# A cross-attention and mixture-of-experts kernel: the next chunk's first key unit moved to the end of each slot

## The chip, the cores and the metric

The kernel runs on one core of one Trainium2 chip. The metric is the device time of one execution in microseconds (us). The core's engines are TensorE (PE in the profile; PEld is its weight load), VectorE (DVE), ScalarE (ACT), GpSimd (POOL) and SyncE (SP), which here only issues DMAs.

## The reference, cut to what matters

```python
x = x + xattn(layernorm(x), ctx, ctx, mask, ...)   # x (64, 128, 128), ctx (64, 120, 128), 16 heads of 8
x = x + ffn(layernorm(x), Wr, W1, b1, W2, b2)       # 8 experts, hidden 512, best 2 of 8 by softmax

def xattn(q_in, k_in, v_in, mask, ...):
    q, k, v = (split_heads(t @ W + b) for ...)
    score = einsum('bhqd,bhkd->bhqk', q, k) / sqrt(8)
    attn = softmax(where(mask, -1e30, score), axis=-1)
    return merge_heads(attn @ v) @ Wo + bo
```

## The kernel before

The work has two phases. The first, up to about 570 us, is attention, the router, and the sorting of rows to experts. The second (the tiles of the expert network) and the final sum are not touched by the change.

**Chunks and slots.** The 64 sequences are taken two at a time: 32 chunks. All engines walk through the same list of slots, `for s in range(-2, 34)`, written out in full. In slot n an engine works on several chunks at once: chunk c = n+1 has its keys and queries projected and the largest score of each query found; chunk n gets its exponentials and its product with the values; chunk n-1 gets its second half's output and the router's logits; chunk n+2 is loaded, normalised and split. The order within a slot is the order of the code on each engine; each engine runs its queue strictly in that order and the engines meet by semaphores.

**A chunk's projections.** There are four units: `project(c, 0)` and `project(c, 1)` make the keys of head groups 0, 1 and 2, 3; `project(c, 2)` and `(c, 3)` make the queries. Each is six matmuls (L1208 to L1210, fp32 split in a high and a low part) into one of three PSUM banks (`wide[u % 3]`) that the scores use too. On ACT `halve(c, u)` (L1039) scales and shifts the bank into `part`. On DVE `unsplit(c, u)` (L695) subtracts `part` from the bank; the result goes to `ks` (keys) or `qs` (queries). When `unsplit` of units 0 and 1 is done, SP copies `ks` in four DMAs (L346, `kb<-ks`) into the block layout `kb`. Only when those have landed can `by_query(c, 0)` (L1247) make the first scores of chunk c, from which DVE takes the maxima (`best`, L700).

**The end of a slot.** After the eighth product with the values (`weigh`, L1269) PE transposes the maxima (L1373) when the last `best` is done; DVE negates and splits them (L868, L870) and SP sends them to a row of `qb` (L365), which the next slot's first `by_key` (L1257) waits for. PE then makes the router's logits (L1381), from which DVE takes the best experts (L878 to L884), and ACT the exponentials `tope` (L1114). DVE also ends the row positions of the router (`posi`, L777), on which POOL's next scatter (L531) waits. ACT's `take_heads(s, 1)` (L1130) copies the second half's heads out of PSUM to `ots1`; the next slot's `turn_heads(s, -1)` on PE (L1229) transposes that copy and so waits for it.

**The start of a slot on PE**: `project(c, 0)`, `turn_heads`, `project(c, 1)`, `turn_on` (L1234, waits for DVE's L660 and L664), `project(c, 2)`, `by_key` twice.

**POOL** runs in each slot, in order: the scatter that waits for `posi`, the mask pair (L556), the output bias, a scatter, the split of chunk n+2's context (L570, L572), a root, a scatter, and in slots 3 to 18 also the split of expert weights (L590, L592).

Of the kernel before, what the change touches and what calls it, by code (L numbers as in the profile page):

```python
# [51 lines left out]
def moe_attention(nc, x, ctx, mask, maskT, Wq, bq, Wk, bk, Wv, bv, Wo, bo, Wr, W1, b12, W2, out):  # L52
# [24 lines left out]
    with ExitStack() as st:  # L77
# [210 lines left out]
        def exists(s, back):  # L288

            return s is None or 0 <= s + back < NCH  # L290
# [345 lines left out]
        def _(dve):  # L636
# [39 lines left out]
            def slot(s, n):  # L676
                c = s + 1
# [4 lines left out]
                    dve.wait_ge(b_full, s.count(8))  # L682
                    dve.wait_ge(pv_done, s.count(8))

                def unsplit(u):

                    dve.wait_ge(w_part, c.count(4, u + 1))
                    gs = slice(2 * (u % 2), 2 * (u % 2) + 2)
                    if u < 2:
                        views = ks[k][:, gs, :], *(w[:, 0:2 * KW].rearrange("p (g n) -> p g n", g=2)[:, :, 0:K2]  # L690
                                                   for w in (wide[u % 3], part[u % 2]))
                    else:
                        views = qs[k][:, :, gs, :], *(w[:, 0:2 * N2].rearrange("p (g b q) -> p b g q", g=2, b=2)
                                                      for w in (wide[u % 3], part[u % 2]))
                    v.tensor_tensor(*views, ALU.subtract).then_inc(w_free, 1)  # L695
# [86 lines left out]
                    normalise((s, -1), False)  # L782
                route(0)
                if exists(n, 1):
                    unsplit(0)
                    route(1)
                    unsplit(1)
                    if n == 0:
                        output_bias()
                else:  # L790
                    route(1)
# [29 lines left out]
                    dve.wait_ge(ln_chain, (s + 3).count(LN, 2))  # L821
                    v.tensor_scalar(ve[:, :], mv[:, :, 1], EPS, None, ALU.add).then_inc(ln_chain, 1)  # L822
                if exists(n, 1):
                    unsplit(2)
                    unsplit(3)
                if exists(n, 2):
                    f = s + 2
                    dve.wait_ge(hx_done, f.count(1, 1))
# [35 lines left out]
                if exists(n, 1):  # L864

                    dve.wait_ge(nm_full, c.count(1, 1))
                    nsrc = small[0][0:J * G * 2, 0:S]
                    v.tensor_scalar(negm[k][:, 0, :], nsrc, -1.0, None, ALU.mult).then_inc(nm_split, 1)  # L868
                    dve.wait_ge(nm_split, c.count(2, 1))
                    v.scalar_tensor_tensor(negm[k][:, 1, :], nsrc, -1.0, negm[k][:, 0, :], ALU.mult, ALU.subtract).then_inc(nm_split, 1)  # L870
                if exists(n, -1):

                    alone(dve, rl_full, s.count(1))
                    lg = small[1][:, 0:2 * E].rearrange("p (b e) -> p b e", b=2)
                    if n != 1:
                        alone(dve, routed, s.count(1, -1))
                    for b in range(2):
                        last = v.max(top[:, b, :], lg[:, b, :])  # L878
                    last.then_inc(top_max, 1)
                    alone(dve, top_max, s.count(1))  # L880
                    for b in range(2):
                        last = v.max_index(tidx[:, b, :], top[:, b, :], lg[:, b, :])
                    last.then_inc(rl_taken, 1)
                    v.tensor_tensor(topd[:], top[:], top[:, :, 0:1].to_broadcast([P, 2, E]), ALU.subtract).then_inc(top_sub, 1)  # L884
# [120 lines left out]
        def _(act):  # L1005
# [3 lines left out]
            def clear(blocks, spec):  # L1009
                dst = flat(blocks, spec).rearrange("p (a n) -> p a n", a=8)  # L1010
                return dst, zeros[:, 0:dst.shape[2]].rearrange("p (a n) -> p a n", a=1).to_broadcast(list(dst.shape))
# [38 lines left out]

            def slot(s, n):
                c = s + 1
                if exists(n, 1):
                    halve(c, 0, n)
                    halve(c, 1, n)
                if exists(n, -1):
                    take_on(s, -1)
                for t in range(8):
                    if t < 7:
                        exponentials(s, t, n)  # L1060
                    if t == 6:
                        if exists(n, -1):
                            m = s + -1
                            act.wait_ge(ln_chain, (s + 3).count(7, 7))
                            if exists(n, -2):
                                act.wait_ge(x2t_full, s.count(1, -1))
                            if exists(n, -5):
                                act.wait_ge(scat[m.phase], m.turns(64, -64))
                            for b in range(2):
                                last = a.activation(rows[m.phase][:, b, 0, 0:D], xres[:, 2 * n - 2 + b, :], ACT.Identity,  # L1070
                                                    bias=shift[:, 2 + b:3 + b], scale=ys[1][:, 2 + b:3 + b])
                            last.then_inc(ln2_done, 1)
                        if exists(n, 3):
                            norm_x(s, n)
                        exponentials(s, 7, n)
                    if t in (0, 1) and exists(n, 1):
                        halve(c, t + 2, n)
                    if t == 4 and exists(n, 0):
                        take_heads(s, 0, n)
                    if t == 2 and exists(n, 1):  # L1080
                        if n == -1:
                            act.wait_ge(vs_zero, 4)
                        act.wait_ge(v_full, c.count(1, 1))
                        if n is None or n >= 1:
                            act.wait_ge(pv_done, s.count(8))
                        a.activation(vs[c.parity][:, :, :, 0:DH].rearrange("p b h d -> p (b h) d"),
                                     small[0][0:KL, 0:2 * D].rearrange("p (b h d) -> p (b h) d", b=2, h=H), ACT.Copy).then_inc(v_taken, 1)
                    if t == 2 and exists(n, 2):

                        f = s + 2  # L1090
                        act.wait_ge(tx_full, f.count(1, 1))
                        if n is None or n >= 0:
                            act.wait_ge(w_full, s.count(12, 4))
                        elif n == -2:
                            act.wait_ge(one_set, 1)
                        a.activation(xcTh[f.parity][:, 0:N2], small[1][:, 0:N2], ACT.Identity, bias=one[:, 0:1]).then_inc(hx_done, 1)
                    if t == 6 and exists(n, 0):
                        take_on(s, 0)
                    if t == 6 and exists(n, -1):

                        act.wait_ge(x2t_full, s.count(1))
                        if n != 1:
                            act.wait_ge(rl_full, s.count(1, -1))
                        a.activation(x2s[:, :], small[0][:, 0:N2], ACT.Copy).then_inc(x2t_taken, 1)
                if n == -2:
                    a.activation(*clear(qb[0], "p b g j q"), ACT.Copy).then_inc(blk_zero, 1)
                if n == -1:
                    a.activation(*clear(kb[1], "p g j n"), ACT.Copy).then_inc(blk_zero, 1)
                    a.activation(*clear(qb[1], "p b g j q"), ACT.Copy).then_inc(blk_zero, 1)
                if exists(n, 0):  # L1110
                    take_heads(s, 1, n)
                if exists(n, -1):
                    act.wait_ge(top_sub, s.count(1))
                    a.activation(tope[:].rearrange("p b e -> p (b e)"), topd[:].rearrange("p b e -> p (b e)"), ACT.Exp).then_inc(top_exp, 1)  # L1114
# [62 lines left out]
        def _(pe):  # L1177
# [58 lines left out]
            def project_out(s, k):  # L1236
                pe.wait_ge(ont_taken, s.count(2, k + 1))
                t_.matmul(small[1][:, 0:D], onT[:, :], wraw[:, 3, :], start=True, stop=True).then_inc(wo_full, 1)
# [34 lines left out]
            def slot(s, n):  # L1273
                c = s + 1
                if n == NCH + 1:
                    turn_x(At(-1, 3), -1, 1)
                if exists(n, 1):
                    project(c, 0, n)
                if n == 0:
                    output_bias()  # L1280
# [19 lines left out]
                for t in range(8):  # L1300
# [61 lines left out]
                        last.then_inc(x2t_full, 1)  # L1362
                    if exists(n, 0) and t == 6:
                        project_out(s, 0)
                    if exists(n, 1) and t == 7:
                        pe.wait_ge(w_free, c.count(12, 12))
                        if n == -1:
                            pe.wait_ge(v_taken, 1)
                        elif n == 0:
                            pe.wait_ge(on_done, 1)  # L1370
                        else:
                            pe.wait_ge(x2t_taken, s.count(1))
                        t_.transpose(small[0][0:J * G * 2, 0:S], mx[:].rearrange("p b g j -> p (b g j)"), ident[:, :]).then_inc(nm_full, 1)  # L1373
# [111 lines left out]
```

## Time and profile before

| | |
|---|---|
| time, median of 3 runs | 906.77 us (905.45 to 907.99) |
| time of the profiled execution | 904.83 us |
| span of the profiled execution | 903.0 us |
| PE busy | 760.7 us (84%) |
| DVE busy | 670.0 us (74%) |
| ACT busy | 621.2 us (69%) |
| POOL busy | 477.3 us (53%) |

The span is the time from the first to the last instruction of the profiled execution; 1.8 us more lie around it in the time measured. A busy share is a mean over stages that are limited in different ways, so it doesn't say what a change within a slot is worth.

### The profile page before, as it was taken

The numbers are of one execution on the slowest core, as the hardware profiler recorded it, in microseconds if no ns is written. First come the engines' busy times: TensorE is split into PE (matmuls) and PEld (weight loads), VectorE is DVE, ScalarE is ACT, GpSimd is POOL, SyncE is SP. The second block draws the span as 40 slices with busy tenths as digits, with TensorE's granted clock in tenths as the row PEclk, the third lists the DMA queues.
The fourth block names the chain that finished last, engine by engine and source line by source line (L and its number), as shares of the span: only waits on it lengthen the run. The fifth ranks groups of instructions, "written<-read, shape, count | busy, mean of one in ns | idle before, by whom it ended". The sixth has DMA issues, their size and how long they took to land.

```text
span 903.0 us, 19629 instructions
## 1 busy us (share of the span) xinstructions
PE 760.7 (84%) x5606; PEld 546.5 (61%) x5606; DVE 670.0 (74%) x2133; ACT 621.2 (69%) x1131; POOL 477.3 (53%) x715
## 2 busy tenths in 40 slices
PE   2689899998998988889988889759999999999700
PEld 1456555655655655656665665448888888888500
DVE  3568888888888887888887887557777777777536
ACT  4667677677677676667776677458888888888500
POOL 4122665565565565454453453453777777767720
PEclk9599999999999999999999999759999999999955
DMA  5333355455445445334243233388877777877059
GB/s 157 75 83 73 98 129 150 115 135 153 115 127 154 116 130 145 102 93 100 72 100 92 70 85 80 141 281 274 253 250 236 254 240 244 243 225 246 19 205 353
DMA packets 117887, 140.33 MB, mean 155 GB/s; under 512 B 20431, under 2 KB 76134, under 8 KB 117799
## 3 DMA queue, kind: packets, MB, share of 16 engines
q1 hardware_dynamic: 105079, 115.72, 45.6%
q0 software_dynamic: 9088, 17.07, 5.4%
q10 hardware_dynamic: 3632, 6.49, 1.9%
q8 instruction: 41, 0.67, 0.3%
q14 instruction: 47, 0.39, 0.1%
HBM read 73.40 MB, written 36.08 MB: 121 GB/s over the span
## 4 chain that ended last, share of the span: by engine, by line
PE 52%; DMA 14%; DVE 13%; SPq 10%; ACT 4%; issue 4%; POOL 1%; POOLq 0%; DVEq 0%; ACTq 0%
DMA kb<-ks 9%; SPq L346 9%; PE bank L1247 6%; DVE mx L700 5%; PE bank L1269 4%; PE bank L1415 4%; PE bank L1412 4%; PE bank L1429 4%; PE bank L1413 4%; PE bank L1427 4%; PE bank L1428 4%; PE bank L1229 3%; DVE ks L695 3%; DMA qb<-yd 3%; PE bank L1257 2%
## 5 line engine op out<-in xcount | busy, mean ns | idle before, releaser
L630 POOL DMA_INDIRECT yd<-vs,idt x156 | 164.9, 1057 | 79.5 <-DVE vs L978 41.0
L1048 ACT ACTIVATE pt<-bank,mpair 120x512 f32<-120x512 f32 x256 | 172.2, 688 | 42.5 <-PE bank L1257 42.3
L531 POOL DMA_INDIRECT xd<-rows,posi x128 | 130.6, 1020 | 127.4 <-DVE posi L777 73.0
L700 DVE TENSOR_REDUCE mx<-bank 128x4 f32<-128x480 f32 x256 | 157.7, 648 | 38.4 <-PE bank L1247 38.2
L964 DVE TENSOR_TENSOR qb<-hid,qb 128x512 fp32r<-128x512 f32 x156 | 109.4, 702 | 68.3 <-ACT hid L1164 67.0
L1161 ACT ACTIVATE qb<-bank,btile 128x512 fp32r<-128x512 f32 x156 | 107.6, 690 | 34.0 <-PE bank L1429 25.0
L1247 PE MATMUL bank<-kb,qs 128*128 128x480 f32 x256 | 96.7, 431 | 35.9 <-DMA kb<-ks 24.9
L1269 PE MATMUL bank<-pt,vs 120*32 120x128 f32 x2048 | 111.4, 290 | 13.3 <-ACT pt L1048 10.3
L1257 PE MATMUL bank<-qb,ks 128*120 128x512 f32 x256 | 118.3, 482 | 2.6 <-DMA qb<-negm 2.6
L1164 ACT ACTIVATE hid<-bank,btile 128x512 f32<-128x512 f32 x156 | 106.3, 681 | 0.0
L1247 PEld LDWEIGHTS bank<-kb,qs 128*128 128x128 f32 x256 | 47.3, 194 | 72.0 <-DMA kb<-ks 34.5
L1269 PEld LDWEIGHTS bank<-pt,vs 120*32 120x32 f32 x2048 | 41.7, 109 | 61.8 <-ACT pt L1048 35.4
L598 POOL TENSOR_SCALAR rows<-rows 128x256 f32<-128x256 f32 x32 | 13.0, 407 | 113.2 <-ACT rows L1070 113.2
L1257 PEld LDWEIGHTS bank<-qb,ks 128*120 128x120 f32 x256 | 44.8, 184 | 44.0 <-issue 39.5
L1130 ACT ACTIVATE ots<-bank 128x512 f32<-128x512 f32 x64 | 38.3, 598 | 40.8 <-PE bank L1269 40.6
L1039 ACT ACTIVATE part<-bank,liftq,rowselq 128x512 fp32r<-128x512 f32 x64 | 49.6, 775 | 15.0 <-PE bank L1210 14.8
L537 POOL TENSOR_TENSOR y<-ve,minus_half 128x4 f32<-128x4 f32 x36 | 37.4, 1040 | 34.1 <-DVE ve L822 31.9
L1039 ACT ACTIVATE part<-bank,liftk,rowselk 128x480 fp32r<-128x480 f32 x64 | 47.3, 743 | 9.9 <-PE bank L1210 9.7
L695 DVE TENSOR_TENSOR ks<-bank,part 128x480 fp32r<-128x480 f32 x64 | 41.8, 653 | 10.3 <-ACT part L1039 9.5
L695 DVE TENSOR_TENSOR qs<-bank,part 128x512 fp32r<-128x512 f32 x64 | 42.2, 681 | 4.8 <-ACT part L1039 4.6
L1208 PE MATMUL bank<-xcTh,wqhi 128*128 128x256 f32 x128 | 39.1, 306 | 4.6 <-DVE ks L695 4.6
L1208 PE MATMUL bank<-xcTh,wkhi 128*128 128x256 f32 x128 | 42.3, 331 | 0.0
(200 smaller groups left out, 1940.1 us busy)
## 6 DMA issues: line engine op xcount, KB each, us to landing
kb<-wd SPq DMA_DIRECT2D x40, 512.0 KB, 5.1
qb<-wd SPq DMA_DIRECT2D x38, 512.0 KB, 5.0
qb<-qs SPq DMA_DIRECT2D x128, 112.0 KB
kb<-ks SPq DMA_DIRECT2D x128, 105.0 KB
rows<-xd SPq DMA_DIRECT2D x39, 264.0 KB, 2.8
wd<-wsp SPq DMA_DIRECT2D x16, 512.0 KB, 3.8
qb<-yd SPq DMA_DIRECT2D x16, 512.0 KB, 6.0
xd<-zrows SPq DMA_DIRECT2D x8, 528.0 KB, 4.6
```

The lines of the kernel that those rows point to most:

```text
L531: g.indirect_dma_start(xd, bass.IndirectOffsetOnAxis(ap=posi[r.phase][:, bk:bk + 1], axis=0), rows[r.phase][:, bk // 2, bk % 2, :], None, ...
L630: g.indirect_dma_start(yd, bass.IndirectOffsetOnAxis(ap=idt[k][:, j:j + 1], axis=0), yrow[p.parity][:, j, :], None, bounds_check=2 * NTOK ...
L695: v.tensor_tensor(*views, ALU.subtract).then_inc(w_free, 1)
L700: v.tensor_reduce(mx[:, b, gg, :], wide[(4 + u) % 3][:, 0:J * KL].rearrange("p (j k) -> p j k", j=J), op=ALU.max, axis=AX.X).then_inc(w_fr ...
L964: v.tensor_tensor(hhl[:, 1, c, :], hid[:, c % 2, :], hhl[:, 0, c, :], ALU.subtract).then_inc(h_lo, 1)
L1039: a.activation(dst, src, ACT.Identity, bias=lift[1 - u // 2][:, 0:1], scale=rowsel[1 - u // 2][:, 0:1]).then_inc(w_part, 1)
L1048: a.activation(pt[t % NP][:].rearrange("p j q -> p (j q)"), scores[t % 2][0:KL, :], ACT.Exp, bias=mpair[s.parity][:, t // G:t // G + 1], s ...
L1161: a.activation(hhl[:, 0, c, :], bank[c][:, :], ACT.Gelu, bias=bias).then_inc(h_hi, 1)
L1164: a.activation(hid[:, c % 2, :], bank[c][:, :], ACT.Gelu, bias=bias).then_inc(h_val, 1)
L1247: t_.matmul(wide[(4 + u) % 3][:, 0:J * KL].rearrange("p (j k) -> p j k", j=J), qs[c.parity][:, b, g, :], kb[c.parity][:, g, :, b * KL:(b + ...
L1257: t_.matmul(scores[t % 2][0:KL, :].rearrange("p (j q) -> p j q", j=J), ks[s.parity][:, g, b * KL:(b + 1) * KL], qb[s.parity][:, b, g, :, : ...
L1269: last = t_.matmul(heads[R * j:R * j + R, g * S:(g + 1) * S], vs[s.parity][:, b, G * g + j, :], pt[t % NP][:, j, :], start=True, stop=True ...
```

## The change

The unit 0 of the next chunk's keys is made at the end of the slot before. On PE its six matmuls stand between the eighth `weigh` and the transposition of the maxima. On ACT its `halve` stands after the copy `x2s` and ahead of `take_heads(s, 1)`. On DVE its `unsplit` stands behind the split of the maxima (L870), with a new wait for the chunk's last `by_key` (the keys of chunk n, in the same buffer, must have been read). Slot -1 still makes its own unit 0 at its start, for chunk 0. So 31 units move, from the start of slots 0 to 30 to the end of slots -1 to 29. No instruction is added or removed.

```diff
-                def unsplit(u):
+                def unsplit(c, u):
+                    k = c.parity
...
                 if exists(n, 1):
-                    unsplit(0)
+                    if n == -1:
+                        unsplit(c, 0)
                     route(1)
-                    unsplit(1)
+                    unsplit(c, 1)
...
                     v.scalar_tensor_tensor(negm[k][:, 1, :], nsrc, -1.0, negm[k][:, 0, :], ALU.mult, ALU.subtract).then_inc(nm_split, 1)
+                if exists(n, 2) and n >= -1:
+                    if n >= 0:
+                        dve.wait_ge(b_full, s.count(8, 8))
+                    unsplit(c + 1, 0)
...
                 c = s + 1
+                if n == -1:
+                    halve(c, 0, n)
                 if exists(n, 1):
-                    halve(c, 0, n)
                     halve(c, 1, n)
...
+                if exists(n, 2) and n >= -1:
+                    halve(c + 1, 0, n + 1)
                 if exists(n, 0):
                     take_heads(s, 1, n)
...
-                if exists(n, 1):
+                if n == -1:
                     project(c, 0, n)
...
                     if exists(n, 0) and t == 6:
                         project_out(s, 0)
+                    if exists(n, 2) and n >= -1 and t == 7:
+                        project(c + 1, 0, n + 1)
                     if exists(n, 1) and t == 7:
                         pe.wait_ge(w_free, c.count(12, 12))
```

ACT's queue where slot 15 ends and slot 16 begins, before. `part0` is the `halve` of unit 0, `part1` that of unit 1, `ots1` is `take_heads(s, 1)`.

```order
L1104 ACTIVATE x2s<-bank6 128x256
L1130 ACTIVATE ots1<-bank5 128x512
L1114 ACTIVATE tope<-topd 128x16
L1039 ACTIVATE part0<-bank0,liftk,rowselk 128x2x240
L1039 ACTIVATE part1<-bank1,liftk,rowselk 128x2x240
```

The same place after the change (the lines of the code are numbered anew):

```order
L1111 ACTIVATE x2s<-bank6 128x256
L1045 ACTIVATE part0<-bank0,liftk,rowselk 128x2x240
L1139 ACTIVATE ots1<-bank5 128x512
L1123 ACTIVATE tope<-topd 128x16
L1045 ACTIVATE part1<-bank1,liftk,rowselk 128x2x240
```

The `halve` of unit 0 now stands ahead of the copy of the heads, where it stood two places behind it.

PE's queue at the same place, before. The six matmuls of unit 0 (into `bank0`) follow the logits; `turn_heads` (`ots1`) comes next.

```order
L1269 MATMUL bank5<-pt3,vs1 32x128 x4
L1373 MATMUL bank6<-ident,mx 32x128
L1381 MATMUL bank7<-wrT,x2s 128x8 x2
L1208 MATMUL bank0<-xcTh1,wkhi 128x256
L1209 MATMUL bank0<-xcTl1,wkhi 128x256
L1210 MATMUL bank0<-xcTh1,wklo 128x256
L1208 MATMUL bank0<-xcTh1,wkhi 128x256
L1209 MATMUL bank0<-xcTl1,wkhi 128x256
L1210 MATMUL bank0<-xcTh1,wklo 128x256
L1229 MATMUL bank6<-ident,ots1 128x128 x4
```

And after:

```order
L1278 MATMUL bank5<-pt3,vs1 32x128 x4
L1217 MATMUL bank0<-xcTh1,wkhi 128x256
L1218 MATMUL bank0<-xcTl1,wkhi 128x256
L1219 MATMUL bank0<-xcTh1,wklo 128x256
L1217 MATMUL bank0<-xcTh1,wkhi 128x256
L1218 MATMUL bank0<-xcTl1,wkhi 128x256
L1219 MATMUL bank0<-xcTh1,wklo 128x256
L1384 MATMUL bank6<-ident,mx 32x128
L1392 MATMUL bank7<-wrT,x2s 128x8 x2
L1238 MATMUL bank6<-ident,ots1 128x128 x4
```

The unit stands ahead of the transposition and the logits; nothing is left between the logits and `turn_heads`.

DVE's queue from the split of the maxima into the next slot, before. `ks0<-bank0,part0` is the `unsplit` of unit 0.

```order
L870 SCALAR_TENSOR_TENSOR negm1<-bank6,negm1 32x128
L878 MAX top<-bank7 128x8 x2
L882 MAX_INDEX tidx<-top,bank7 128x8 x2
L884 TENSOR_TENSOR topd<-top 128x16
L772 TENSOR_REDUCE posf<-placed 128x4
L777 CAST posi0<-posf 128x4
L660 RECIPROCAL rden<-bank6 128x16
L664 TENSOR_TENSOR on<-bank6,rden 128x128
L729 CAST pick<-tidx 128x4
L695 TENSOR_TENSOR ks0<-bank0,part0 128x480
```

And after:

```order
L872 SCALAR_TENSOR_TENSOR negm1<-bank6,negm1 32x128
L696 TENSOR_TENSOR ks0<-bank0,part0 128x480
L884 MAX top<-bank7 128x8 x2
L888 MAX_INDEX tidx<-top,bank7 128x8 x2
L890 TENSOR_TENSOR topd<-top 128x16
L773 TENSOR_REDUCE posf<-placed 128x4
L778 CAST posi0<-posf 128x4
L660 RECIPROCAL rden<-bank6 128x16
L664 TENSOR_TENSOR on<-bank6,rden 128x128
```

The router's best experts and `posi` now stand behind the `unsplit`.

## Rows read from the trace of the kernel before

**Rows 1.** The chain that ended last, slot 16: start, us, what.

```profile
314.68 0.76 ACT part L1039
315.46 0.67 DVE ks L695
...
318.85 2.49 DMA kb<-ks
...
321.38 0.50 PE bank L1247
```

**Rows 2.** Timeline of PE, slots 15 and 16: start, us, [idle before <-releaser].

```profile
311.80 0.09 PEld L1373 LDWEIGHTS bank<-ident,mx 128*32 128x32 f32 x1 [0.23 <-DVE mx L700]
311.83 0.27 PE L1373 MATMUL bank<-ident,mx 128*32 128x128 f32 x1
312.54 0.36 PE L1208 MATMUL bank<-xcTh,wkhi 128*128 128x256 f32 x1
313.21 0.28 PE L1210 MATMUL bank<-xcTh,wklo 128*128 128x256 f32 x1
313.33 0.60 PE L1229 MATMUL bank<-ident,ots 128*128 128x128 f32 x4
314.36 0.28 PE L1210 MATMUL bank<-xcTh,wklo 128*128 128x256 f32 x1
...
328.94 0.27 PE L1373 MATMUL bank<-ident,mx 128*32 128x128 f32 x1
```

**Rows 3.** Timeline of ACT, the same boundary.

```profile
311.91 0.60 ACT L1130 ACTIVATE ots<-bank 128x512 f32<-128x512 f32 x1 [0.23 <-PE bank L1269]
313.49 0.22 ACT L1114 ACTIVATE tope<-topd 128x16 f32<-128x16 f32 x1 [0.98 <-DVE topd L884]
313.61 0.73 ACT L1039 ACTIVATE part<-bank,liftk,rowselk 128x480 fp32r<-128x480 f32 x1
```

**Rows 4.** Views of L710 and L753: count, ns min/median/max, first to last start.

```profile
L710 DVE TENSOR_TENSOR yy<-y x14: 436/930/1274, 99.3 to 322.6; 128x4 f32<-128x4 f32 x14
...
L710 DVE TENSOR_TENSOR yy<-y x10: 151/152/152, 375.2 to 527.4; 128x4 f32<-128x4 f32 x10
...
L753 DVE TENSOR_TENSOR taken<-taken x18: 137/372/526, 112.5 to 405.0; 128x8 bf16<-128x8 bf16 x18
```

**Rows 5.** Timeline of POOL and DVE, slot 16.

```profile
314.56 0.97 POOL L531 DMA_INDIRECT xd<-rows,posi  x1 [2.89 <-DVE posi L777]
321.45 0.64 POOL L590 TENSOR_SCALAR wsp<-hid 128x512 fp32r<-128x512 f32 x1
321.98 0.66 DVE L700 TENSOR_REDUCE mx<-bank 128x4 f32<-128x480 f32 x1 [0.88 <-PE bank L1247]
322.18 1.28 POOL L592 TENSOR_TENSOR wsp<-hid,wsp 128x512 fp32r<-128x512 f32 x1
322.55 0.93 DVE L710 TENSOR_TENSOR yy<-y 128x4 f32<-128x4 f32 x1
```

**Rows 6.** Timeline of PE, the same transposition in slots 23 and 24.

```profile
447.46 0.27 PE L1373 MATMUL bank<-ident,mx 128*32 128x128 f32 x1
...
463.85 0.27 PE L1373 MATMUL bank<-ident,mx 128*32 128x128 f32 x1
```

**Rows 7.** Timeline of DVE, the same boundary.

```profile
312.72 0.25 DVE L878 MAX8 top<-bank 128x8 f32<-128x8 f32 x2
...
313.59 0.17 DVE L777 CAST posi<-posf 128x4 int32<-128x4 f32 x1
314.13 0.26 DVE L660 RECIPROCAL rden<-bank 128x16 f32<-128x16 f32 x1 [0.37 <-PE bank L1229]
```

**Rows 8.** Timeline of SP and PE: issue of the maxima, first `by_key`.

```profile
312.76 1.22 SPq L365 DMA_DIRECT2D qb<-negm  x2
...
315.78 0.50 PE L1257 MATMUL bank<-qb,ks 128*120 128x512 f32 x1
```

**Rows 9.** View of line L365, 100 to 500 us.

```profile
DMA to landing us min/median/max: 2.1/2.1/3.1
```

More of the change, by code:

```diff
@@ L823, in slot @@
                 if exists(n, 1):
-                    unsplit(2)
-                    unsplit(3)
+                    unsplit(c, 2)
+                    unsplit(c, 3)
                 if exists(n, 2):
```

## The prediction

> **What bounds the kernel now.** I read the chain of waits first. In the slots it goes around one loop, and the same rows return slot after slot: the end of `project(c, 1)` releases ACT's `halve` (314.68), that releases DVE's `unsplit` (315.46), that the `kb<-ks` DMAs, whose last part of 2.49 us starts at 318.85, and their landing releases the first scores at 321.38 [rows 1]. From there it goes over the maxima and the PE queue to the transposition at 328.94, and round again. One turn is 328.94 - 311.83 = 17.11 us [rows 2]. So whatever stands on PE between the transposition and the end of `project(c, 1)` is on the path, and whatever is late there makes every slot longer. A wait for the DMAs that ends last can't absorb it, since the DMAs start later too.
>
> Then I read the timelines of PE, ACT and DVE across one boundary. The reader is to see in PE's that nothing stands between the rows: transposition 311.83, unit 0 from 312.54, its last matmul 313.21, `turn_heads` 313.33 [rows 2]. In ACT's: `take_heads` ends at 311.91 + 0.60 = 312.51, 0.8 us before PE comes to it, and then ACT stands idle for 0.98 us [rows 3].
>
> There is a second thing. In slots 3 to 16 the DVE multiplication L710 takes 0.93 us instead of 0.15 [rows 4]: it starts behind the first maxima and ends with POOL's L592 (322.18 + 1.28 = 323.46) [rows 5]. The next maxima wait for it. Without it a turn takes 463.85 - 447.46 = 16.39 us [rows 6], with it 17.11; about 0.75 us of DVE stall goes through to the time.
>
> **The change part by part.** *PE, unit 0.* 313.33 - 312.54 = 0.79 us of matmuls go from behind the logits to ahead of the transposition. The sum of PE's work between the eighth `weigh` and the end of unit 1 stays the same, so by itself this is worth nothing. PE's weight load of the transposition stood idle for 0.23 us [rows 2]; unit 0 doesn't wait for the last maxima and could use at most that. I take 0, since the load of the transposition comes right behind the eighth `weigh` anyway; bounds 0 and 0.23 of gain. Unit 0's other inputs are early: the context's split stands in POOL's queue ahead of L590 at 321.45 [rows 5], 7 us before the slot's end. The new wait on DVE for the last `by_key` costs nothing either: PE has issued it ahead of the eighth `weigh`.
>
> *ACT, `halve(c+1, 0)` ahead of `take_heads`.* This is the cost. Unit 0's last matmul comes at 313.21 - 0.71 = 312.50. `halve` follows such a matmul by 314.68 - 314.36 = 0.32 us [rows 1, 2], so it runs from 312.82 to 313.55 (0.73 [rows 3]). Queued behind it is `take_heads`, 0.60 us: 313.57 to 314.17. PE comes to `turn_heads` at 313.33, as before, and now has to wait. With 0.12 us from ACT's end to PE's start (an estimate; bounds 0.03 and 0.2) it starts at 314.29, not 313.33: **+0.96 us**. With the bounds above it is 0.64 to 1.04. Nothing covers it: `project(c, 1)` stands behind `turn_heads` in PE's queue, and its `halve`, `unsplit` and DMAs are the chain.
>
> *ACT and DVE behind it.* `unsplit(c+1, 0)` waits for the `halve`, 313.55, and for the negation; the transposition starts 0.79 later, 312.62, and the maxima are ready 312.76 - 311.83 = 0.93 later [rows 2, 8], also 313.55. It takes 0.67 [rows 1], so L878 starts at 314.22 instead of 312.72 [rows 7], and `posi` and `topd` are 1.50 later as well. `tope` goes to 313.49 + 1.50 = 314.99 and ends at 315.21; behind it on ACT is the `halve` of unit 1, due at 314.68 + 0.96 = 315.64, so 0.43 us of cover is left. DVE's L777 ends at 315.26 and L660 starts at about 315.28 instead of 314.13, 1.15 later. The `unsplit` of unit 1 doesn't feel that, since unit 0 no longer stands between; `turn_on`, the query units and `by_key` come 0.2 us later than the 0.96, which PE's idle time ahead of the first scores takes up.
>
> *The DMA of the maxima.* Issue 313.55, the second about 0.6 later, landing 2.1 after that, 316.3 (3.1 at worst: 317.3) [rows 8, 9]. `by_key` stood at 315.78 and moves to about 316.9. Covered, but only because `turn_heads` is late: without that, PE would wait 0.5 us there. `posi` being late holds POOL's scatter, and with it POOL's whole queue, next.
>
> *POOL against DVE.* L531 waits for `posi` [rows 5], and POOL works without a pause of note from there to L592, so its queue moves by 1.50 and DVE's maxima by 0.96. L592 then ends at 323.46 + 1.50 = 324.96. L710 comes at 321.98 + 0.66 + 0.96 = 323.60, L592 starts at 323.68: L710 may slip in ahead. But the addition L763 two places behind it also reads two SBUF tensors, as L753 does, and L753 too is stretched, from 0.137 to a median of 0.372 us, when POOL works [rows 4]. So the stall isn't lost, it moves to L763, and the second maxima start behind L592 either way: 1.50 later, not 0.96. That is +0.54 in 14 slots. Bounds: the stall vanishes (-0.75 each), or L710 is held and nothing more (0).
>
> *Sum.* `take_heads` exists at 30 of the moved places (slots 0 to 29): 30 x 0.96 = 28.8. In slots 3 to 16: 14 x 0.54 = 7.6. At slot -1's end ACT has no `take_heads` and I count nothing (a gain of at most the 0.79 of unit 0). Together +36.4 us, on the profiled execution's 904.83: 941.2; the median of the runs is 1.9 us above that execution, so **943 us**.
>
> **The rivals.**
> 1. *`take_heads` as above, the stall stays the same size.* 906.8 + 28.8 = 935.6. For it: the phases differ by tenths. Against: L592 ends the wait, and L592 is late by more than DVE.
> 2. *The stall is dodged.* DVE passes L710 and L763 before L592 takes hold: 28.8 - 14 x 0.75 = 18.3, so 925. For it: L710 is due 0.08 us ahead of L592. Against: L763 isn't. It needs POOL another 0.3 us late.
> 3. *Only a permutation.* ACT isn't late at `turn_heads` and the time stays 907. It needs the `halve` to be ready at once, against 0.32 + 0.73 us read.
> 4. *Faster.* The place is L710 and L763 again: freed of L592, they give back 14 x 0.75 = 10.5 us, and the time is 896 if the boundary costs nothing. It decides once a boundary costs under 10.5 / 30 = 0.35 us. My low bound for it is 0.64.
> 5. *Slower than forecast.* The 0.43 us of cover on ACT is used up: `tope` waits for DVE, and every tenth past it delays unit 1's `halve` at each of 30 boundaries. 0.3 us beyond it give 9 more, 952 us.
>
> **How the numbers follow.** Forecast 0.42; rival 1 0.20; rival 2 0.15; rival 3 0.05; rival 4 0.06; rival 5 0.12. The forecast's own range is 936 to 949 (0.1 us either way per boundary, and part of the 0.54). From 921 to 954 the cases left out are rivals 3 and 4 and half of rival 5, under 2 in 10. A change of 0.3% (2.7 us) is about what a measurement of this kernel tells from none. Faster: rival 4, 0.06; same: most of rival 3, 0.04; slower: all the rest, 0.90.
>
> **What would show it.** In the profile after: PE idle of about 1 us before L1229's successor at each slot's start, ended by ACT's `ots`, 30 times; `ots` starting right behind `part0`; the loop running over that copy in the chain of waits; 17.3 to 17.4 us a turn in slots 19 on, 18.6 in slots 3 to 16; L763's successor stretched to some 1.1 us and L710's short. I am wrong if `turn_heads` starts without a wait, if `by_key` waits for `qb<-negm`, or if the chain goes over `tope`.

## The result, and the profile after

The changed kernel takes 942.58 us (median of 4 runs, 938.11 to 943.92), the kernel before on the same chips 906.11 (4 runs, 904.01 to 907.99). The ratio is 1.0384, with a 95% interval from 1.0338 to 1.0429. In the runs further down some executions take over 1.5% longer than the fastest of the same kernel; medians count them, ratios leave them out. Taken again later it gave 942.21 against 907.15 (1.0374, 1.0322 to 1.0427).

The page of the changed kernel, its first line and the busy times:

```profile
span 940.1 us, 19659 instructions
...
PE 761.3 (81%) x5606; PEld 549.2 (58%) x5606; DVE 675.6 (72%) x2133; ACT 624.2 (66%) x1131; POOL 477.3 (51%) x715
```

Each engine does as many instructions as before; the total was 19629, and the 30 more are as many as the new wait on DVE adds (slots 0 to 29). The span grows by 940.1 - 903.0 = 37.1 us. The view of the windows says where: here cut at the first and the last transposition of the maxima, first the kernel before, then the one after. Columns: stretch and length, then busy time of PE, PE's weight loads, DVE, ACT and POOL, the granted clock, the DMA share and GB/s.

```profile
35.12:565.84 530.72, 476.12 (x4190) 318.16 (x4190) 431.39 (x1649) 376.74 (x734) 267.66 (x420) 0.99 0.42 108
565.84:903.00 337.16, 271.86 (x1377) 219.14 (x1375) 221.67 (x422) 228.94 (x376) 198.15 (x259) 0.89 0.71 232
```

```profile
35.36:600.54 565.18, 472.85 (x4185) 317.88 (x4183) 436.94 (x1649) 379.50 (x734) 267.24 (x420) 0.99 0.40 102
600.54:940.10 339.56, 274.36 (x1377) 220.71 (x1375) 221.70 (x422) 228.87 (x376) 198.65 (x259) 0.88 0.72 230
```

The slots take 565.18 - 530.72 = 34.5 us more, at the same clock (0.99), while PE's busy time does not grow: it waits. DVE's busy time grows by 436.94 - 431.39 = 5.5 us with the same 1649 instructions: some of them are held up, which counts as busy. The 5.5 are the balance of several such instructions and not the price of one: `hot` (L741) and `before` (L764) are busy 9.8 and 7.5 us longer than before the change, `yy` (L711), `ve` and `taken` 6.1, 4.4 and 4.4 us shorter. The part behind the slots is 2.4 us longer; in the second profile of the same kernel it is 337.1, so I don't put that to the change.

One boundary of slots in the timeline of the changed kernel, the one of [rows 2], [rows 3], [rows 7] and [rows 8]. The last matmul of unit 0 now starts at 331.84, ahead of the transposition at 331.95.

```profile
331.84 0.28 PE L1219 MATMUL bank<-xcTh,wklo 128*128 128x256 f32 x1
...
331.95 0.27 PE L1384 MATMUL bank<-ident,mx 128*32 128x128 f32 x1
...
332.15 0.75 ACT L1045 ACTIVATE part<-bank,liftk,rowselk 128x480 fp32r<-128x480 f32 x1 [1.10 <-PE bank L1219]
...
332.81 0.59 ACT L1139 ACTIVATE ots<-bank 128x512 f32<-128x512 f32 x1
...
333.54 0.63 PE L1238 MATMUL bank<-ident,ots 128*128 128x128 f32 x4 [0.96 <-ACT ots L1139]
333.58 0.24 DVE L884 MAX8 top<-bank 128x8 f32<-128x8 f32 x2
...
334.34 0.22 ACT L1123 ACTIVATE tope<-topd 128x16 f32<-128x16 f32 x1 [0.95 <-DVE topd L890]
334.44 0.17 DVE L778 CAST posi<-posf 128x4 int32<-128x4 f32 x1
...
334.91 0.75 ACT L1045 ACTIVATE part<-bank,liftk,rowselk 128x480 fp32r<-128x480 f32 x1 [0.35 <-PE bank L1219]
```

The reader is to see the queue on ACT: the `halve` at 332.15, right behind it `ots` at 332.81, where in [rows 3] `ots` started ahead of the logits. PE has nothing left to do and waits for it, by 0.96 us. `tope` is not in the way: ACT is idle for 0.35 us ahead of the `halve` of unit 1. The view of the waits over all slots has the same wait 30 times. Its first line is POOL's wait for `posi`, which took 73.0 us in 27 times before the change (line, releaser: us in total, times, longest):

```profile
POOL xd L531 <- DVE posi L778: 108.9, 26, 4.4
...
PE bank L1238 <- ACT ots L1139: 29.3, 30, 1.3
```

And it lies on the chain that ended last, at the place where [rows 1] has only the release of `part` by PE:

```profile
332.81 0.59 ACT ots L1139
333.40 0.14 issue
333.54 0.63 PE bank L1238 x4
...
343.07 1.10 DVE before L764
```

The last of these is the second cost. The timeline of POOL and DVE in that slot answers to [rows 5] (L711 is L710 of the kernel before, L764 is L763, L701 is L700):

```profile
342.26 0.66 DVE L701 TENSOR_REDUCE mx<-bank 128x4 f32<-128x480 f32 x1 [0.78 <-PE bank L1256]
342.83 0.15 DVE L711 TENSOR_TENSOR yy<-y 128x4 f32<-128x4 f32 x1
342.88 1.28 POOL L592 TENSOR_TENSOR wsp<-hid,wsp 128x512 fp32r<-128x512 f32 x1
342.99 1.19 DVE L764 TENSOR_TENSOR before<-before,taken 128x8 bf16<-128x8 bf16 x1
344.10 0.64 DVE L701 TENSOR_REDUCE mx<-bank 128x4 f32<-128x480 f32 x1
```

L711 slips in 0.05 us ahead of POOL's subtraction, L764 doesn't: its 1.19 us end when POOL's 1.28 us do, and the second maxima start there. The next transposition is at 350.24, so this turn is 350.24 - 331.95 = 18.29 us, against 17.11. Where POOL has no subtraction, the turn is that of these two rows (for [rows 6]), 17.28 against 16.39:

```profile
458.20 0.27 PE L1384 MATMUL bank<-ident,mx 128*32 128x128 f32 x1
...
475.48 0.27 PE L1384 MATMUL bank<-ident,mx 128*32 128x128 f32 x1
```

### The profile page after: what moved, and what is told of

Its sections match the earlier page's. It is cut to its first block, busy times and chain, and to the rows that moved or that the text cites. A ratio compares the mean times of both kernels' runs of the same rounds, so it can differ in the third digit from the quotient of the medians.

```text
span 940.1 us, 19659 instructions
## 1 busy us (share of the span) xinstructions
PE 761.3 (81%) x5606; PEld 549.2 (58%) x5606; DVE 675.6 (72%) x2133; ACT 624.2 (66%) x1131; POOL 477.3 (51%) x715
## 3 DMA queue, kind: packets, MB, share of 16 engines
q0 software_dynamic: 9088, 17.07, 5.3%
## 4 chain that ended last, share of the span: by engine, by line
PE 49%; DMA 15%; DVE 12%; SPq 11%; issue 6%; ACT 6%; POOL 1%; POOLq 0%; DVEq 0%; ACTq 0%
SPq L346 9%; DMA kb<-ks 9%; PE bank L1256 6%; DVE mx L701 5%; PE bank L1278 4%; PE bank L1426 4%; PE bank L1423 4%; PE bank L1424 4%; PE bank L1438 4%; PE bank L1440 4%; PE bank L1439 4%; PE bank L1238 3%; DMA qb<-yd 3%; ACT part L1045 3%; PE bank L1266 2%
## 5 line engine op out<-in xcount | busy, mean ns | idle before, releaser
L701 DVE TENSOR_REDUCE mx<-bank 128x4 f32<-128x480 f32 x256 | 157.7, 648 | 38.0 <-PE bank L1256 37.9
L1170 ACT ACTIVATE qb<-bank,btile 128x512 fp32r<-128x512 f32 x156 | 107.5, 689 | 34.2 <-PE bank L1440 25.9
L1238 PE MATMUL bank<-ident,ots 128*128 128x128 f32 x256 | 40.6, 283 | 29.4 <-ACT ots L1139 29.3
L1238 PEld LDWEIGHTS bank<-ident,ots 128*128 128x128 f32 x256 | 30.4, 144 | 34.1 <-DVE negm L872 31.5
```

The costliest lines, as they stand in the source:

```text
L701: v.tensor_reduce(mx[:, b, gg, :], wide[(4 + u) % 3][:, 0:J * KL].rearrange("p (j k) -> p j k", j=J), op=ALU.max, axis=AX.X).then_inc(w_fr ...
L1170: a.activation(hhl[:, 0, c, :], bank[c][:, :], ACT.Gelu, bias=bias).then_inc(h_hi, 1)
L1238: last = t_.transpose(small[0][:, g * P:(g + 1) * P], ots[k % 2][:, g, :], ident[:, :])
```

## The experiments

There were eleven more runs, in three groups. In the first two (the first eight below) the kernel before itself took 947 and 946 us, and in the traces of those eight the part behind the last transposition takes 368 to 386 us instead of 337: 377 to 384 where the kernel before was edited, 368 to 386 where the change was, so this isn't the change's. So they are read in the slots, by the trace: the phase from the first to the last transposition of the maxima, the median turn between two transpositions that begins in slots 3 to 17 (with POOL's subtraction), and the median of the quiet turns that begin in slots 21 to 24, without it. All in us:

| kernel | phase | turn, slots 3 to 17 | quiet turn |
|---|---|---|---|
| before | 530.7 | 17.13 | 16.37 |
| the change | 565.2 | 18.34 | 17.27 |
| the change again | 564.0 | 18.46 | 17.26 |
| change, `halve` behind the heads | 551.2 | 17.67 | 17.07 |
| change, `unsplit` back | 556.1 | 17.82 | 17.27 |
| PE's part of the change alone | 546.0 | 17.69 | 16.66 |
| before, POOL's split later | 529.7 | 16.81 | 16.39 |
| before, POOL's split early | 522.6 | 16.56 | 16.39 |
| the same again | 524.1 | 16.46 | 16.40 |
| change, POOL's split early | 550.1 | 17.38 | 17.28 |
| before, fourth `kb` DMA on ACT | 525.1 | 17.13 | 16.42 |
| before, both | 519.1 | 16.45 | 16.44 |
| the same again | 515.6 | 16.46 | 16.46 |

The granted clock in the slots (35 to 550 us) is 0.97 to 1.00 in all of them. Where one kernel was traced twice, the phases differ by 1.2, 1.4 and 3.5 us, so a difference of that size tells nothing; the kernel before has one trace. A turn in slots 3 to 17 less a quiet turn is called the stall below; it is what POOL's subtraction costs: 17.13 - 16.37 = 0.76 before, 18.34 - 17.27 = 1.07 in the change.

**1. The `halve` behind `take_heads`.** The changed kernel, with the two exchanged on ACT; PE and DVE as in the change.

```diff
-                if exists(n, 2) and n >= -1:
-                    halve(c + 1, 0, n + 1)
                 if exists(n, 0):
                     take_heads(s, 1, n)
+                if exists(n, 2) and n >= -1:
+                    halve(c + 1, 0, n + 1)
```

> The change, but on ACT the moved halve stands behind take_heads instead of ahead of it. My theory (the wait at turn_heads comes from this order on ACT): PE no longer waits for ots, turn_heads follows the logits at once. Not all of the loss goes away: tope still waits for the router's results, which stand behind the moved unsplit on DVE and come 1.4 us late, so unit 1's halve starts 0.55 us late, and by_key about 0.65; with POOL's weight split pushed onto a later DVE instruction in 15 slots 0.8 there: 15 x 0.65 + 15 x 0.8 = 22, about 928 us. Rival (the order on ACT doesn't matter, the loss comes from the late maxima and posi): the time stays near 942.

Measured: 970.51 us, ratio 1.0262 (1.014 to 1.0384). The wait of PE for `ots` is gone from all boundaries, and the phase is 14.0 us shorter than that of the change. But the quiet turn gets only 0.20 us back, and stays 0.70 above before. The greater part of the 14.0 lies in the stall, which is 17.67 - 17.07 = 0.60 here: in 11 of the 16 slots POOL's subtraction comes so late that both L711 and L764 are through, and L714, the next instruction with two SBUF inputs, is held for 0.7 us instead. The timeline of this kernel at a quiet boundary:

```profile
446.81 0.60 ACT L1139 ACTIVATE ots<-bank 128x512 f32<-128x512 f32 x1 [0.72 <-PE bank L1278]
...
447.00 0.27 PE L1384 MATMUL bank<-ident,mx 128*32 128x128 f32 x1
...
447.30 0.74 ACT L1045 ACTIVATE part<-bank,liftk,rowselk 128x480 fp32r<-128x480 f32 x1
...
447.95 0.66 PE L1238 MATMUL bank<-ident,ots 128*128 128x128 f32 x4 [0.34 <-DVE negm L872]
...
449.49 0.22 ACT L1123 ACTIVATE tope<-topd 128x16 f32<-128x16 f32 x1 [1.44 <-DVE topd L890]
449.61 0.73 ACT L1045 ACTIVATE part<-bank,liftk,rowselk 128x480 fp32r<-128x480 f32 x1
```

Two other waits stood right behind the one removed. PE has to wait 0.34 us for the split of the maxima (`negm`), which reads the bank that `turn_heads` writes. And ACT stands idle for 1.44 us until `topd` comes, which DVE makes behind the `unsplit` of unit 0; only then the `halve` of unit 1 starts. That is the loop over `tope`, here for real. So `take_heads` is the longest of three waits at this place, not the only one.

**2. The `unsplit` back at the slot's start.** The changed kernel; DVE's part alone is taken back.

```diff
                 if exists(n, 1):
-                    if n == -1:
-                        unsplit(c, 0)
+                    unsplit(c, 0)
...
-                if exists(n, 2) and n >= -1:
-                    if n >= 0:
-                        dve.wait_ge(b_full, s.count(8, 8))
-                    unsplit(c + 1, 0)
```

> The change, but DVE's unsplit of unit 0 is back at the start of the slot; PE's unit and ACT's halve stay moved. My theory: the wait at turn_heads stays (0.9 us at 30 boundaries), while posi and the router's results are late by only 0.8 instead of 1.4, so POOL's weight split ends 0.8 late: 15 x 0.9 + 15 x 0.8 = 25.5, about 932 us. Rival (the moved unsplit is what costs): near 910.

Measured: 968.22 us, ratio 1.0153 (0.998 to 1.0325). The phase is 556.1. PE's wait for `ots` is untouched, and the quiet turn with it (17.27). In the timeline, a boundary and the POOL subtraction behind it:

```profile
164.07 0.63 PE L1233 MATMUL bank<-ident,ots 128*128 128x128 f32 x4 [0.96 <-ACT ots L1134]
...
172.77 1.28 POOL L592 TENSOR_TENSOR wsp<-hid,wsp 128x512 fp32r<-128x512 f32 x1
...
173.30 0.77 DVE L711 TENSOR_TENSOR yy<-y 128x4 f32<-128x4 f32 x1
```

With `posi` 0.8 us earlier again, the subtraction starts ahead of L711, and L711 is the one that is held, as in [rows 5]; the turn in the slots with a subtraction falls by 0.52, from 18.34 to 17.82. The first cost is all there and the second is gone: the stall, 17.82 - 17.27 = 0.55, is even below the 0.76 of before. Counted from the eighth `weigh`, medians over the slots with a subtraction, L592 starts 0.69 us later than before and the first maxima 0.92: POOL now loses less than DVE. In the change it was 1.36 against 0.97, and there the stall grew. So the second cost goes by the difference of the two delays; `posi` behind the `unsplit` gives about half of POOL's.

**3. PE's part alone.** `project(c + 1, 0)` ahead of the transposition, the `halve` and the `unsplit` at the slot's start as before (in the diff of the change, ACT's and DVE's lines are taken back).

```diff
-                if n == -1:
-                    halve(c, 0, n)
                 if exists(n, 1):
+                    halve(c, 0, n)
                     halve(c, 1, n)
...
-                if exists(n, 2) and n >= -1:
-                    halve(c + 1, 0, n + 1)
                 if exists(n, 0):
                     take_heads(s, 1, n)
```

> Only PE's six matmuls are moved; halve and unsplit stand where they stood before. My theory: no wait at turn_heads. The maxima and the logits are 0.79 us later, tope with them, and unit 0's halve stands behind tope on ACT, so unit 1's halve is about 0.55 late; POOL 0.79 late in 15 slots: 15 x 0.55 + 15 x 0.79 = 20, about 926 us. Rival (moving PE's work is a permutation and costs nothing): 906.

Measured: 960.63 us, ratio 1.0162 (0.9981 to 1.0343). The phase is 546.0, 15.3 above before, so this part alone isn't free. The quiet turn is 0.29 longer. The timeline at such a boundary:

```profile
461.36 0.66 PE L1230 MATMUL bank<-ident,ots 128*128 128x128 f32 x4 [0.34 <-DVE negm L871]
...
461.98 0.22 ACT L1115 ACTIVATE tope<-topd 128x16 f32<-128x16 f32 x1 [1.15 <-DVE topd L885]
...
462.10 1.41 ACT L1040 ACTIVATE part<-bank,liftk,rowselk 128x480 fp32r<-128x480 f32 x2
```

Unit 0's matmuls had covered the time that DVE needs for `negm`. Gone from there, they leave PE idle for 0.34 us. I had costed PE's part at nothing. The stall is 17.69 - 16.66 = 1.03 here, nearly that of the change, with DVE's part taken back as in run 2: L592 is 0.70 us later than before, the first maxima only 0.53. So the second cost doesn't hang on DVE's part alone. PE's part delays `posi` as well, since it puts the transposition and with it `negm` and the logits later.

**4. Before, with POOL's split later.** The kernel before; its split of the expert weights (L590 and L592) stands behind the slot's last scatter.

```diff
-                if n in WUNITS:
...
-                    g.tensor_tensor(wsp[:, 1, w, :], hid[:, w, :], wsp[:, 0, w, :], ALU.subtract).then_inc(wsplit, 1)
                 if exists(n, -1):
...
                     scatter(s + -3, (3,))
+                if n in WUNITS:
...
+                    g.tensor_tensor(wsp[:, 1, w, :], hid[:, w, :], wsp[:, 0, w, :], ALU.subtract).then_inc(wsplit, 1)
```

> The kernel before, with POOL's split of expert weights (L590, L592) moved from ahead of the row copies to behind them, where POOL waited for posi. My theory (DVE instructions with two SBUF inputs wait for POOL, 0.75 us in 15 slots, on the path): the multiplication yy takes 0.15 us everywhere, turns of 16.4 us instead of 17.1, less up to 0.3 where topd now meets the split: about 897 us (895 to 901). Rival (the stall is off the path): 906.

Measured: 949.03 us, ratio 1.0042 (0.9976 to 1.0108): no difference that can be told. No maxima are held any more, but the turn is 16.81, not 16.4. The timeline at a boundary:

```profile
309.10 0.65 DVE L767 TENSOR_TENSOR placed<-hot,place 128x16 f32<-128x16 bf16 x2
...
310.10 0.58 PE L1381 MATMUL bank<-wrT,x2s 128*128 128x8 f32 x4 [0.40 <-DVE xres L674]
...
310.45 1.29 POOL L604 TENSOR_TENSOR wsp<-hid,wsp 128x512 fp32r<-128x512 f32 x1
...
311.30 0.48 DVE L884 TENSOR_TENSOR topd<-top 128x16 f32<-128x16 f32 x1
```

The split now stands some 7 us later and collides with DVE's work at the boundary: `placed` takes 0.65 instead of 0.25 and `topd` 0.48 instead of 0.15, `xres` comes late and PE waits 0.40 us at the logits. The stall had moved again.

**5. Before, with POOL's split early.** The same two instructions ahead of the slot's square root, so that they run while DVE has slack.

```diff
                     g.tensor_tensor(xcTl[k][:, tc], xcT[k][:, tc], xcTh[k][:, tc], ALU.subtract).then_inc(hl_done, 1)
+                    if n in WUNITS:
...
+                        g.tensor_tensor(wsp[:, 1, w, :], hid[:, w, :], wsp[:, 0, w, :], ALU.subtract).then_inc(wsplit, 1)
                     if n is None or exists(n, 3) or exists(n, -1):
```

> The kernel before, with POOL's split of expert weights ahead of the root instead of behind it. There DVE has only instructions with a PSUM input (the query unsplits), so by my theory none waits for it: yy takes 0.15 us everywhere, turns of 16.4 us instead of 17.1 in slots 3 to 17, 15 x 0.72 = 11 us less than before, provided the root, now 2 us later, is still ready when yy is due. Rival (the root becomes the wait: yy is held by it as long as it was by the split): no gain, within 0.3% of before.

Measured: 936.91 us, ratio 0.987 (0.9753 to 0.9988). The turn in slots 3 to 17 falls to 16.56, close to the quiet one, and no instruction of DVE among the maxima is held. The phase is 8.1 us shorter, where 11 were expected.

**6. The change, with POOL's split early.** The same edit in the changed kernel, which leaves the boundary's cost alone. The expectation calls the kernel of run 5 e8.

> The change, with the same move of POOL's weight split. My theory: of the change's two costs only the wait at turn_heads is left: 0.9 us at 30 boundaries over the e8 kernel, so about 27 us more than that one, and some 8 us less than the change; turns of 17.3 us in all slots. Rival (POOL's queue is late enough that the root holds yy here): turns of 17.8 or more in slots 3 to 17.

Measured: 973.87 us, ratio 1.0366 (1.027 to 1.0461). The phase is 550.1 - 522.6 = 27.5 us above that of run 5, which differs by the change only: 0.92 per boundary over 30 (26.0 and 0.87 against the second trace of run 5's kernel). It is also 15.1 us below that of the change, where 8 were expected: the edit takes away what the stall cost before, and what the change had added to it. In the timeline the wait is as before, and L711 is short:

```profile
164.82 0.63 PE L1238 MATMUL bank<-ident,ots 128*128 128x128 f32 x4 [0.96 <-ACT ots L1139]
...
174.17 0.16 DVE L711 TENSOR_TENSOR yy<-y 128x4 f32<-128x4 f32 x1
```

**7. Before, with the fourth `kb` DMA on ACT.** SP issues the four `kb<-ks` DMAs one after the other, and they are on the chain. The fourth goes to ACT's queue, behind `take_on(s, -1)`.

```diff
-                        for j in range(J):
+                        for j in range(J - 1 if blocks is kb else J):
...
+                if exists(n, 1):
+                    act.wait_ge(w_free, c.count(12, 2))
...
+                    act.dma_start(dst[:, :, j, :].bitcast(F32), src.bitcast(F32)).then_inc(kblk[c.parity], 16)
                 for t in range(8):
```

> The kernel before, with the last of the four kb<-ks DMAs issued by ACT, behind its copy of the output, instead of as the fourth by SP. My theory (the loop runs over SP's serial issues, 0.86 us each): the keys land up to 0.8 us earlier and PE's idle time ahead of the first scores, 0.5 us a turn, goes: up to 15 us less. Rival (ACT's issue holds the first exponential by 0.6 us, for which PE waits): no gain, or up to 5 us lost.

Measured: 942.98 us, ratio 1.0001 (0.9943 to 1.0059). The phase is 5.6 us shorter, but neither kind of ordinary turn is (17.13 and 16.42). What went is the few long turns: before has one of 19.32 us in slot 26, this kernel one of 16.43 there.

**8. Before, with both.** Runs 5 and 7 together.

> The kernel before with both moves: POOL's weight split ahead of the root and the fourth kb DMA on ACT. If both theories hold the gains add, as the one frees DVE and the other PE's wait: 20 to 26 us less than before. If the rival of the DMA move holds: the gain of the split's move alone.

Measured: 935.46 us, ratio 0.9946 (0.9892 to 1.0001); the phase, 519.1, is the shortest of this group, 11.6 us under before. The 20 to 26 us of the first theory aren't there; of the fourth DMA only its effect on the long turns is left.

**9. The change again**, on a chip where the expert part runs as in the first measurement, beside the next two.

> The change itself, once more beside the kernel before on one chip. The attention phase (first to last transposition of maxima) should take 34 to 35 us more than before's 530.7, turns of 18.3 us in slots 3 to 17 and 17.3 in the quiet late ones, and the part behind it as long as before: its 2.4 us more in the first pair of traces is by my theory not the change's. Rival: the part behind is longer again by 2 us or more.

Measured: 942.21 us (6 runs, 938.36 to 945.48) against 907.15 (11 runs, 902.80 to 914.95), ratio 1.0374. The span of the profile is 937.1, the phase 564.0, 33.3 above before where 34 to 35 were expected. The part behind is as long as before (337.1), so its rival fails.

**10. Before, split early, again.**

> The kernel before with POOL's weight split ahead of the root, again: 8 us less in the attention phase, about 0.9% less time. Rival: the gain in the phase is given back by the experts' loads and the time is within 0.3% of before.

Measured: 897.89 us (895.68 to 899.21), ratio 0.9879 (0.9832 to 0.9927). The timeline of POOL and DVE in a slot:

```profile
162.85 1.28 POOL L581 TENSOR_TENSOR wsp<-hid,wsp 128x512 fp32r<-128x512 f32 x1
...
165.73 0.15 DVE L710 TENSOR_TENSOR yy<-y 128x4 f32<-128x4 f32 x1
```

The subtraction is over at 162.85 + 1.28 = 164.13, 1.6 us before L710 begins, and L710 takes its own 0.15 us. The place is worth 907.15 - 897.89 = 9.3 us of the kernel before by the medians, and 903.0 - 896.3 = 6.7 by the spans of the two profiles.

**11. Before, with both, again.**

> The split ahead of the root and the fourth key DMA on ACT, again: the turn is the same as without the DMA move (16.4 us), so the same time as the kernel with the split's move alone, 0 to 3 us less. Rival (the move helps the slots with a late DMA): 5 us less than that kernel.

Measured: 888.97 us (888.33 to 891.03), ratio 0.9789 (0.9742 to 0.9835). It beats both kernels, and run 10 by 8.9 us, 8.5 of them in the slots (515.6 against 524.1). The rival is what held here. The quiet turn didn't shrink (16.46 against 16.40), which the timeline explains:

```profile
140.76 2.67 SPq L346 DMA_DIRECT2D kb<-ks  x3
140.77 0.82 ACTq L1066 DMA_DIRECT2D kb<-ks  x1
...
141.71 0.69 ACT L1048 ACTIVATE pt<-bank,mpair 120x512 f32<-120x512 f32 x1 [1.50 <-PE bank L1266]
...
142.45 0.43 PE L1278 MATMUL bank<-pt,vs 120*32 120x128 f32 x8 [1.10 <-ACT pt L1048]
```

ACT's issue of the DMA takes 0.82 us, and the first exponential stands behind it: PE waits 1.10 us at the first `weigh`. What SP saves at one end is paid at the other. But the turns that were long for a late landing are gone: the first turn apart, which is over 20 us in both, run 10 still has three of 18.5 to 18.9 us, with waits of 1.3 to 1.6 us for the landing instead of 0.6, and this kernel none above 17.11. The views of the waits of both, the first line run 10's, the second this one's (in total, times, longest):

```profile
PE bank L1247 <- DMA kb<-ks: 25.9, 27, 3.1
```

```profile
PE bank L1256 <- DMA kb<-ks: 3.0, 3, 2.2
```

The wait for the landing, 25.9 us in 27 slots, is left in three of them. That the last of the four DMAs now comes in parallel is the plain reading; whether the long turns came from the queue or from contention of transfers was not taken apart.

## Why the prediction was right

The forecast was 943.0, the time 942.58. The mechanism was that of the forecast: PE waits for ACT's late copy at 30 boundaries, and POOL's subtraction holds DVE for longer. But both terms came out smaller than forecast, 32.0 us together instead of 36.4, and that the total is right to half a microsecond is luck: the difference is filled by 2.5 us of long turns and 2.4 us behind the slots, which the forecast did not have.

- *`take_heads` late at `turn_heads`: +0.96 forecast.* PE's wait is 0.96 in the row and 29.3 / 30 = 0.98 in the mean, but the shift of `turn_heads` is 0.84 and that of a quiet turn 0.90 (17.27 - 16.37). I had ACT's copy start 0.75 us after the `halve`; it starts 332.81 - 332.15 = 0.66 after it. PE follows `ots` by 0.14; the estimate was 0.12. Thirty boundaries cost 30 x 0.90 = 27.0, not 28.8; run 6 gives 26.0 to 27.5 by itself.
- *PE's part costs nothing: wrong taken alone, right in the sum.* Run 3 shows 0.34 us of wait for `negm` (0.29 on the quiet turn). In the change it lies under the longer wait for `ots`.
- *`posi` +1.50: +1.48 measured. L592 +1.50: +1.33* (each against the row of before, moved by the start of the eighth `weigh`). *The second maxima +1.50: +1.17 to 1.21.* So the stall adds 18.34 - 17.13 - 0.90 = 0.31 per slot, not 0.54, but in 16 slots rather than 14: 5.0 us, not 7.6. Sixteen is the number of POOL's subtractions; the 14 are one row of L710 in [rows 4]. In the kernel before a fifteenth (slot 18) is held too, and in slot 17 DVE came too late to be held.
- *The stall moves to L763 (now L764): half right.* It does in 7 of the 16 slots, where L711 slips in by hundredths as in the rows above. In 7 more L711 itself is still held, since in those slots the first maxima come 0.1 to 1.0 us later against POOL's subtraction, in most behind first scores that are late. In 2 both pass, and L714, one place on, is held for some 0.7 us; those are the cheap turns, 17.75 and 17.84. Which instruction it is depends on hundredths; that one is, doesn't.
- *The rest of the sum.* 27.0 + 5.0 = 32.0 of the 34.5 us. The other 2.5 lie in single long turns outside the slots with a subtraction (19.30 us in slot 1, 16.89 before); they differ between profiles of the same kernel (565.2 and 564.0), and I don't put them to a mechanism.
- *`tope`'s cover of 0.43 holds:* 0.35 of it is left. Run 1 shows it as the next wait, once the `halve` and the `unsplit` come later. *`by_key` is covered:* the waits of PE for `qb<-negm` are 2.3 us in all, against 2.6 before.

Of the rivals, 2 and 4 would have needed the stall dodged. Run 6 dodges it by an edit, and what stays is the 27.5 us of the boundary, far above the 10.5 of the fourth rival. Run 1 shows that a POOL late by some tenths more wouldn't have helped rival 2 either: L711 and L764 pass, and L714 is held. Rival 1, the stall at its old size, fails by little: it is 1.07 against 0.76. Rival 3, only a permutation, fails by the 30 waits, and rival 5 by the 0.35 us of cover that is left.

The rule of the Trainium skill that the prediction drew on (page "SBUF — State Buffer", section "Who interferes with whom") agrees with the runs: in 15 of the 16 slots of the change the instruction held is the first one with two SBUF inputs behind the start of POOL's subtraction, a multiplication of 128x4 or a bf16 addition of 128x8, and the maxima, which read PSUM, pass. The exception is slot 6, where L764 starts 0.02 us behind POOL (158.49 against 158.47) and isn't held, but L714 is. That POOL waits in its turn when DVE is first, these traces don't show. In the row at 342.26 the maxima run beside POOL's start unchanged, 0.66 us.

## What to carry to other kernels

An in-order queue charges a moved instruction to whatever stands behind it: before an instruction is put ahead of another, read when the one behind it is needed, here by PE within 0.1 us. Ask as well what work the moved piece had covered where it stood; the six matmuls had hidden a wait for DVE that is next to nothing among the waits of the kernel before (0.4 us in all, at two weight loads) and 0.34 us at a boundary without them. And a stall between two engines that hold each other up is best removed by a place where the other engine has slack; delays of some tenths only changed the victim and the length of the stall (runs 1 to 3). How far it is moved doesn't decide: some 7 us later it met other work of DVE's at the boundary and gained nothing (run 4), 2.5 us earlier it met instructions that read PSUM and gained 9.3 us (run 10).

## What was not expected of the hardware

- Two ACT instructions in a row overlap at their ends: `ots` starts 0.66 us after a `halve` whose row has 0.75.
- A 128x512 subtraction on POOL of 1.28 us stretches a DVE addition of 128x8 from 0.15 to 1.27 us. Instructions with a single tensor at DVE's input can be longer too: `ve` took from 0.17 to 0.73 us in the kernel before, and where it took 0.49 or more its row ends with that of POOL's subtraction L572 (at 215.54: 0.73 us, L572 ends 0.70 us after its start). Whether POOL is the cause was not taken apart.
- A DMA issued by ACT holds ACT for 0.82 us, as long as SP is held by each of its own (0.81 to 0.90), and PE waited 1.10 us for the exponential behind it. It still paid, 8.9 us, by the long turns that vanished.
